# Two cross-attentions, fourth quarter of a context: another order of the projection units of the next context, and two of its loads and splits at other places

## The chip, the cores and the metric

The kernel runs on one core of one Trainium2 chip. The core has five engines that each work through a queue of their own: TensorE (PE: matmuls, and PEld: their weight loads), VectorE (DVE), ScalarE (ACT), GpSimd (POOL), and SyncE (SP), whose queue issues nearly all DMA transfers. They meet only through semaphores. An engine's queue is strictly in order, so an instruction that waits holds up all that stands behind it. The metric is the device time of one execution in microseconds (us); the median of three runs before is 2287.61 us (2285.31 to 2291.52).

## The reference

Two transformer layers over 8 inputs of 224 rows x 512, with one context of 750 x 512 per input. Each layer has a cross-attention and a feed-forward network, with gates:

```
x = x + tanh(g_xattn[0]) * attention0(layernorm(x), ctx)   # 16 heads of 32, no mask
x = x + tanh(g_ffn[0])   * bit_ffn(layernorm(x))           # ternary weights, depthwise convolution
x = x + tanh(g_xattn[1]) * attention1(layernorm(x), ctx, mask)   # 8 heads of 64, mask
x = x + tanh(g_ffn[1])   * fp4_ffn(layernorm(x))           # weights and activations rounded to FP4

# attention: q = x Wq, k = ctx Wk, v = ctx Wv
# out = softmax(q k^T * d^-0.5 [masked]) v Wo
```

All is float32 in the reference. The kernel keeps that precision with bf16 matmuls: each operand is the sum of a bf16 value (its high part) and a bf16 remainder (its low part), and a product takes three matmuls.

## The kernel before

The four stages run one after the other: attention 0 (to about 750 us), its feed-forward, attention 1 (from about 1130 to 1870 us), its feed-forward. One function, `cross_attention`, writes both attentions; `stacked` is true for attention 0 and false for attention 1. Here b is the number of an input with its context, and both have eight.

**Quarters and slots.** The work on b is cut into four quarters q = 0 to 3, with HC heads each (4 in attention 0, 2 in attention 1). Per head TensorE computes the transposed scores (`scores_t`, L1189) whose exponential feeds the values, the scores of the same head of the next input (`scores`, L1209, in two halves) of which VectorE takes the row maxima (L977, L972), and the values of the head two back (`values`, L1227). Between these stand the *units* that prepare later inputs, four slots per head: slot 0 ahead of `scores_t`, slot 1 behind it, slot 2 behind the values, slot 3 behind the second half of the scores. `quarter_units` lists the units of a quarter and `slots_of` gives each its slot; every engine's code calls both, so that all have the same order.

**Units.** ("X", s, b) transposes half s of the normalised input (L1161). ("K", (c, kh), b), ("Q", c, b) and ("V", j, b) project a chunk of the keys (for half kh of the context), of the queries, and a piece of the values (L1117). "M" transposes maxima, "OT" and "OP" are the output projection. Each unit passes three engines: TensorE computes it in one of two PSUM banks, ScalarE copies out the high part (`unit_hi_part`, L772 to L790), VectorE the low part (`unit_lo_part`), and only then does TensorE reuse the bank. In the fourth quarter of b the units are X, K and Q of b + 2: X(0), X(1), chunk 0 of the keys and of the queries. They are needed at the start of the next quarter, where head 0 of b + 2 gets its first scores.

**Keys and queries take a detour.** A head's rows must lie at other partitions than where the projection leaves them. When K(c, 1) or Q(c) is done, SP writes the chunk to DRAM (L466), waits until it has landed, and reads it back into the stack in three transfers (L476, `regroup`). SP does this unit by unit, in the order of the units. `scores` waits, at the first head of a quarter, for all six reads of its chunk (`st_in`).

**The context.** In attention 0 a context comes in two halves of 375 columns through one float32 buffer (L416, 750 KB). ScalarE rounds a half to bf16 (`split_ctx`, L737, waits for the load) and VectorE computes the remainders chunk by chunk (`split_chunk`, L918, at the places in CHUNKS). SP loads the second half behind the queries' regrouping in quarter 2. In attention 1 the halves come ready from DRAM (`load_parts`, L403, 750 KB each).

**ScalarE's other work.** For each head `exponentials` (L801) reads the banks of `scores_t`, and `exponentials_hi` (L811) rounds the result. TensorE may write the next head's transposed scores only when the exponential of the head before has read them (`exp_done`).

**Weight pieces.** Attention 1 also rounds the last stage's weights to FP4, one piece per quarter: SP stores the finished piece (L511) behind K(c, 1) and loads one (L503) behind Q(c).

Of the kernel before, what the change touches and what calls it, by code (L numbers as in the profile page):

```python
# [25 lines left out]
NJ = 6  # L26
# [68 lines left out]
def cross_attention(nc, tag, x_in, x_out, ctx_t, ctx_parts, weights, gate, masks, H, fp4_weights=None, kept=None):  # L95
# [16 lines left out]
    def quarter_units(q, b):  # L112
        kq = b + 1 if q < 3 else b + 2
        cc = (q + 1) % KC
        units = []
        if q == 3 and (b + 2).exists():
            units += [("X", 0, b + 2), ("X", 1, b + 2)]

        maxima = []
        if q == 2 and (b + 1).exists():  # L120
            maxima = [("M", 0, b + 1)]
        if q == 0 and b.exists() and b.number != 0:
            maxima = [("M", 1, b)]
        chunk = [("K", (cc, 0), kq), ("K", (cc, 1), kq), ("Q", cc, kq)] if kq.exists() else []
        if q == 1 and (b + -1).exists():

            units += [("OT", 0, b + -1), ("OT", 1, b + -1)] + chunk + [("OP", 0, b + -1), ("OP", 1, b + -1)]
        else:
            if stacked and q == 3 and chunk:
                units = chunk[:1] + units + [chunk[2], chunk[1]]  # L130
            else:
                units += chunk[:1] + maxima + chunk[1:] if stacked or q == 0 else maxima + chunk
        if (b + 1).exists():
            turn = ((0, 1, 2), (3,), (4, 5), ()) if stacked else ((0, 1), (2,), (3, 4, 5), ())
            units += [("V", j, b + 1) for j in turn[q]]
        return units

    def slots_of(q, b):

        units = quarter_units(q, b)  # L140
        use = (2, 0) if len(units) <= 2 * HC else (2, 0, 1, 3)
        open_slots = sorted(4 * j + k for j in range(HC) for k in use)
        slots = [[] for _ in range(4 * HC)]
        at = [open_slots[i * len(open_slots) // len(units)] for i in range(len(units))]
        if q == 0 and not stacked and units and units[-1][0] == "V":

            at = [0, 1, 2, 3, 6, 7] if len(units) == 6 else [0, 1, 3, 6, 7][5 - len(units):]
        if units and units[0][0] == "OT" and not stacked:
            at[:2] = [0, 1]
        if stacked and q == 3 and units:  # L150

            at = [1, 2, 4, 6, 9]
        for slot, u in zip(at, units):
            slots[slot].append(u)
        return slots
# [19 lines left out]
    with ExitStack() as ctx:  # L175
# [201 lines left out]
        def _(sp):  # L377
# [127 lines left out]
            def weight_pieces(q, b, unit):  # L505

                m = 4 * b.number + q - 2
                if unit[0] == "K" and unit[1][1] == 1 and 1 <= m <= FP4_PIECES:

                    sp.wait_ge(f_rounded, m + 1)  # L510
                    sp.dma_start(fp4_weights[m - 1][1], fw[:, (m - 1) % 2, :]).then_inc(fw_sent, 16)  # L511
                if unit[0] == "Q" and 1 <= m < FP4_PIECES - 1:

                    sp.wait_ge(fw_sent, m * 16)
                    load_weight_piece(m + 1)
# [29 lines left out]
            def quarter(q, b):  # L545
# [24 lines left out]
                for unit in quarter_units(q, b):  # L570
# [4 lines left out]
                        load_ctx(b + 2, 1)  # L575
                    if not stacked and q == 2 and (b + 2).exists():

                        if unit[:2] == ("K", (KC - 1, 1)):
                            load_ctx(b + 2, 0)
                        if unit[:2] == ("V", NJ - 1):  # L580
                            sp.wait_ge(unit_done, value(n))
# [135 lines left out]
        def _(act):  # L717
# [109 lines left out]
            def quarter(q, b):  # L827
# [6 lines left out]
                def unit_step(unit):  # L834
                    unit_hi_part(unit)
                    if stacked and unit[:2] == ("K", (KC - 1, 1)) and (b + 2).exists():
                        split_ctx(b + 2, 0, None)
                    if stacked and unit[:2] == ("K", (0, 0)) and (b + 2).exists():
                        split_ctx(b + 2, 1, None)

                for j in range(HC):
# [17 lines left out]
        def _(dve):  # L859
# [176 lines left out]
            def quarter(q, b):  # L1036
# [16 lines left out]
                for j in range(HC):  # L1053
# [24 lines left out]
                    for unit in slots[4 * j + 3]:  # L1078
                        unit_step(unit)

            CHUNKS = {(2, 3): [(0, 0), (0, 1)], (2, 4): [(0, 2), (0, 3)],
                      (3, 1): [(1, 0), (1, 1)], (3, 2): [(1, 2), (1, 3)]}
            MOMENTS = {(2, 0): 0, (2, 1): 1} if stacked else {(2, 0): 0}
            NORMALISED = {(2, 5): [0], (2, 7): [1]} if stacked else {(2, 2): [0], (2, 3): [1]}

# [16 lines left out]
        def _(pe):  # L1102
# [18 lines left out]
            def unit_products(unit):  # L1121
# [14 lines left out]
                if kind == "M":  # L1136

                    pe.wait_ge(sm_done, (b.index * H + (k + 1) * H2) * 2)
                if kind == "OP" and k == 0 or unit[:2] == ("Q", 0) and stacked and (b.number is None or b.number >= 2):

                    pe.wait_ge(unit_done, n - 1)
                elif not (isinstance(n, int) and n <= 2):
# [1383 lines left out]
```

## Time and profile before

| | |
|---|---|
| median of 3 runs | 2287.61 us (2285.31 to 2291.52) |
| profiled execution, device time | 2280.43 us |
| its span in the trace | 2278.6 us |
| TensorE matmuls / weight loads busy | 1975.2 us (87%) / 1385.9 us (61%) |
| VectorE, GpSimd, ScalarE busy | 1477.8, 1214.7, 949.6 us |
| TensorE granted clock, mean | 0.937 of full speed |

A row of a timeline gives the start in us from the span's start, how long the row lasts, the engine, the line, the operation with its output and inputs, how many instructions are merged in it, and in brackets how long the engine stood idle before it and what released it. Both attentions share names (`a_...`); the weights and keys of attention 1 are called `kept_w` and `kept_k`. A row of the waits gives who waited for whom, the total in us, how often, and the longest. A row of stretches gives each engine's busy time within a stretch, then the granted clock of TensorE, the busy share of the DMA engines, and their GB/s.

### The profile page before, as it was taken

The page shows a single profiled execution, that of the slowest core. Times are in us where ns is not written, and L with a number is a line of the kernel's source. Part 1 is how long each engine was busy: PE and PEld are TensorE (multiplying, and loading weights), DVE is VectorE, ACT ScalarE, POOL GpSimd, SP SyncE. Part 2 cuts the span into 40 slices and gives each one's busy share as a digit, 9 for nine tenths or more (in the row PEclk, how much of TensorE's full clock was granted, in tenths as well). Part 3 has the DMA queues.
Part 4 walks back from the last instruction along what each step waited for, and adds up shares of the span by engine and source line. Part 5 has one row for each costly group of instructions (what it writes and reads, how often), then busy time and mean ns, then how long its engine had stood idle before and what let it go on. Part 6 is the DMA issues. An engine that isn't in the chain of part 4 may idle for free. (4 is left out here: it accounts for less than half of the span.)

```text
span 2278.6 us, 42253 instructions
## 1 busy us (share of the span) xinstructions
PE 1975.2 (87%) x15208; PEld 1385.9 (61%) x15208; DVE 1477.8 (65%) x2752; ACT 949.6 (42%) x1289; POOL 1214.7 (53%) x1470
## 2 busy tenths in 40 slices
PE   5798898898897478989588898998999977899997
PEld 3466666666666367778355676666666664455553
DVE  4766666666656479897454556655656546898973
ACT  3266666666657573333133334334333443111111
POOL 4166666657756453333221556566666422777763
PEclk9899999999999589999788999999999988899998
DMA  7354344344331231111253443434444422011100
GB/s 208 94 123 107 92 108 118 94 112 119 96 92 41 99 97 33 40 32 33 86 162 93 114 124 116 135 118 136 123 127 132 127 83 65 28 33 33 36 23 28
DMA packets 184011, 208.67 MB, mean 92 GB/s; under 512 B 61480, under 2 KB 145704, under 8 KB 183336
## 3 DMA queue, kind: packets, MB, share of 16 engines
q1 hardware_dynamic: 183848, 206.46, 32.0%
q8 instruction: 107, 1.75, 0.3%
q14 instruction: 56, 0.46, 0.1%
HBM read 138.61 MB, written 67.53 MB: 90 GB/s over the span
## 5 line engine op out<-in xcount | busy, mean ns | idle before, releaser
L678 POOL TENSOR_TENSOR a_p_hl<-a_p,a_p_hl 125x448 bf16<-125x448 f32 x540 | 578.7, 1073 | 533.8 <-ACT a_p_hl L811 505.3
L811 ACT ACTIVATE a_p_hl<-a_p 125x1344 bf16<-125x1344 f32 x192 | 254.0, 1323 | 140.4 <-PE a_psum L1227 137.4
L801 ACT ACTIVATE a_p<-a_psum 125x1344 f32<-125x1344 f32 x192 | 247.7, 1290 | 130.5 <-PE a_psum L1189 123.0
L977 DVE TENSOR_REDUCE a_nm<-a_psum 112x1 f32<-112x750 f32 x256 | 236.4, 930 | 24.9 <-PE a_psum L1209 23.0
L1227 PEld LDWEIGHTS a_psum<-a_v_st,a_p_hl 125*128 125x128 bf16 x4608 | 185.4, 100 | 39.7 <-issue 19.7
L1227 PE MATMUL a_psum<-a_v_st,a_p_hl 125*128 125x65 bf16 (+2 forms) x4608 | 196.7, 198 | 9.5 <-ACT a_p_hl L811 3.1
L1209 PE MATMUL a_psum<-a_k_st,a_q_st 96*112 96x375 bf16 x512 | 134.0, 348 | 77.5 <-DVE a_nm L977 72.4
L1856 PE MATMUL f_conv<-f_u,f_taps 128*128 128x224 f32 x768 | 161.6, 360 | 22.2 <-DVE f_u L1708 21.3
L942 DVE TENSOR_TENSOR a_v_st<-a_psum,a_v_st 125x512 bf16<-125x512 f32 x96 | 66.4, 691 | 171.9 <-ACT a_v_st L779 171.9
L1117 PE MATMUL a_psum<-a_chl,kept_w 128*128 128x375 bf16 x768 | 141.9, 339 | 24.4 <-DVE kept_w L868 18.3
L1856 PEld LDWEIGHTS f_conv<-f_u,f_taps 128*128 128x128 f32 x768 | 141.9, 192 | 31.7 <-DVE f_u L1708 27.0
L1209 PE MATMUL a_psum<-kept_k,a_q_st 128*112 128x375 bf16 (+1 forms) x512 | 127.7, 350 | 38.4 <-DMA a_q_st<-a_q 35.6
L1117 PE MATMUL a_psum<-a_chl,a_w 128*128 128x375 bf16 x768 | 140.5, 335 | 18.9 <-DVE a_w L868 14.9
L972 DVE CUSTOM_DVE_ANT_0 a_psum<-a_psum,a_mask_b 112x750 f32<-112x750 f32 x128 | 120.0, 942 | 50.3 <-PE a_psum L1209 48.8
L936 DVE TENSOR_TENSOR a_k_tmp<-a_psum,a_k_tmp 128x375 bf16<-128x375 f32 x128 | 69.8, 545 | 125.5 <-ACT a_k_tmp L772 125.4
L779 ACT ACTIVATE a_v_st<-a_psum 125x512 bf16<-125x512 f32 x96 | 58.4, 608 | 208.7 <-PE a_psum L1117 208.7
L1117 PE MATMUL a_psum<-a_w,a_chl 128*125 128x512 bf16 x576 | 135.7, 386 | 3.2 <-DVE a_q_tmp L939 3.1
L1117 PE MATMUL a_psum<-kept_w,a_chl 128*125 128x512 bf16 x576 | 134.6, 384 | 3.5 <-DVE a_q_tmp L939 3.4
L772 ACT ACTIVATE a_k_tmp<-a_psum 128x375 bf16<-128x375 f32 x128 | 61.9, 484 | 170.8 <-PE a_psum L1117 168.3
L2181 POOL TENSOR_TENSOR f_ht<-f_ht,f_hp 128x512 f32<-128x512 f32 (+1 forms) x84 | 99.1, 1208 | 60.9 <-DVE f_hp L1934 59.8
L1587 ACT ACTIVATE f_t<-f_conv,f_cb 128x224 f32<-128x224 f32 x128 | 57.5, 449 | 167.0 <-PE f_conv L1856 167.0
L1117 PEld LDWEIGHTS a_psum<-a_chl,kept_w 128*128 128x128 bf16 x768 | 74.7, 102 | 79.4 <-issue 38.8
(251 smaller groups left out, 4045.5 us busy)
## 6 DMA issues: line engine op xcount, KB each, us to landing
a_k<-a_k_tmp SPq DMA_DIRECT2D x64, 375.0 KB, 2.9
a_k_st<-a_k SPq DMA_DIRECT2D x96, 187.5 KB, 3.4
kept_k<-a_k SPq DMA_DIRECT2D x96, 187.5 KB, 3.4
a_c<-in_ctx_t SPq DMA_DIRECT2D x16, 750.0 KB, 5.8
ctx_parts<-a_chl SPq DMA_DIRECT2D x16, 750.0 KB, 9.2
a_chl<-ctx_parts SPq DMA_DIRECT2D x16, 750.0 KB, 6.7
a_q_st<-a_q SPq DMA_DIRECT2D x192, 56.0 KB, 2.2
rounded<-a_fw SPq DMA_DIRECT2D x24, 352.0 KB, 3.7
```

The costliest lines, as they stand in the source:

```text
L678: ins = nc.gpsimd.tensor_tensor(p_hl[0:MC, h % 2, 1, cols], p32[0:MC, h % 2, cols], p_hl[0:MC, h % 2, 0, cols], ALU.subtract)
L801: nc.scalar.activation(p32[0:MC, par, :].rearrange("p (b n) -> p b n", b=3), st[0:MC, :, 0:2 * S], ACT.Exp, scale=scale).then_inc(exp_done, 1)
L811: nc.scalar.activation(p_hl[0:MC, par, 0, :], p32[0:MC, par, :], ACT.Copy).then_inc(phi_done, 1)
L936: ins = nc.vector.tensor_tensor(k_tmp[:, cc % 2, 1, cols], bank[:, 0:MK], k_tmp[:, cc % 2, 0, cols], ALU.subtract)
L942: ins = nc.vector.tensor_tensor(v_st[0:MC, b.parity, k, :, DK + 1:VW], bank[0:MC, :].rearrange("p (h d) -> p h d", h=H), v_st[0:MC, b.pari ...
L972: ins = nc.vector.tensor_tensor_reduce(out=sm_[0:HALF, 0:2, 0:MK], in0=sm_[0:HALF, 0:2, 0:MK], in1=mask_b[:, b.parity, s, :].rearrange("p ...
L977: ins = nc.vector.tensor_reduce(out, sm_[0:HALF, 0:2, 0:MK], AX.XY, ALU.max, negate=True)
L1117: ins = nc.tensor.matmul(out, lhs, rhs, start=(c == 0 and n == 0), stop=(c == KC - 1 and n == 2))
L1209: ins = nc.tensor.matmul(sm_[0:HALF, kh, 0:MK], q_stack(b.parity, at(h), rows)[:, s * HALF:(s + 1) * HALF], k_stack(b.parity, at(h), rows) ...
L1227: ins = nc.tensor.matmul(ob[:, c0:c0 + width], p_hl[0:MC, h % 2, part, j * S + Q0[s]:j * S + Q0[s] + P], v_st[0:MC, b.parity, j, h, 0:widt ...
L1856: ins = nc.tensor.matmul(conv[:, g % 2, c * S:(c + 1) * S], taps[:, g * GC + c, k, :], u[:, g % 2, c, k:k + S], start=(k == 0), stop=(k == 2))
L2181: ins = nc.gpsimd.tensor_tensor(ht[:, cols], ht[:, cols], hp[:, cols], op)
```

## The change

Four things move; no computation is added or removed.

- Attention 0, fourth quarter: the units were K(0,0), X(0), X(1), Q(0), K(0,1) and are K(0,0), X(0), K(0,1), X(1), Q(0), at the same slots 1, 2, 4, 6, 9.
- Attention 0: ScalarE's rounding of the second half of the context (L737) stands behind the last V unit of the third quarter, and VectorE's remainders of it one place earlier (behind the first and second maximum of head 12).
- Attention 1, fourth quarter: the units were X(0), X(1), K(0,0), K(0,1), Q(0) at slots 0, 1, 3, 4, 6 and are X(0), X(1), Q(0), K(0,0), K(0,1) at 0, 0, 2, 3, 4. Q(0) then waits until X(1) is wholly out of its bank, as in attention 0.
- Attention 1: SP loads the first half of the next context behind the queries of the third quarter, not behind its keys, and the weight piece that the fourth quarter loaded is loaded in the first quarter of the next, behind its unit K(1,0).

```diff
             if stacked and q == 3 and chunk:
-                units = chunk[:1] + units + [chunk[2], chunk[1]]
+                units = [chunk[0], units[0], chunk[1], units[1], chunk[2]]
+            elif q == 3:
+                units += chunk[2:] + chunk[:2]
             else:
                 units += chunk[:1] + maxima + chunk[1:] if stacked or q == 0 else maxima + chunk
...
+        if not stacked and q == 3 and units:
+
+            at = [0, 0, 2, 3, 4]
...
-                if unit[0] == "Q" and 1 <= m < FP4_PIECES - 1:
+                if q == 0:
+                    if unit == ("K", (1, 0), b + 1) and 2 <= m < FP4_PIECES:
+
+                        sp.wait_ge(fw_sent, (m - 1) * 16)
+                        load_weight_piece(m)
+                if unit[0] == "Q" and q != 3 and 1 <= m < FP4_PIECES - 1:
...
-                        if unit[:2] == ("K", (KC - 1, 1)):
+                        if unit[:2] == ("Q", KC - 1):
                             load_ctx(b + 2, 0)
...
-                    if stacked and unit[:2] == ("K", (0, 0)) and (b + 2).exists():
+                    if stacked and q == 2 and unit[:2] == ("V", NJ - 1) and (b + 2).exists():
                         split_ctx(b + 2, 1, None)
...
-                      (3, 1): [(1, 0), (1, 1)], (3, 2): [(1, 2), (1, 3)]}
+                      (3, 0): [(1, 0), (1, 1)], (3, 1): [(1, 2), (1, 3)]}
...
-                if kind == "OP" and k == 0 or unit[:2] == ("Q", 0) and stacked and (b.number is None or b.number >= 2):
+                if kind == "OP" and k == 0 or unit[:2] == ("Q", 0) and (b.number is None or b.number >= 2):
```

ScalarE in attention 0, from the last V unit of the third quarter (a_v_st) on. Before, the exponential (a_p) and rounding (a_p_hl) of head 11, the exponential of head 12 and K(0,0) (a_k_tmp) come ahead of the rounding of the context (a_chl):

```order
L779 ACTIVATE a_v_st<-a_psum 125x16x32
L796 REGISTER_ALU
L801 ACTIVATE a_p<-a_psum 125x1344
L807 REGISTER_ALU
L811 ACTIVATE a_p_hl<-a_p 125x1344
L796 REGISTER_ALU
L801 ACTIVATE a_p<-a_psum 125x1344
L765 REGISTER_ALU
L772 ACTIVATE a_k_tmp<-a_psum 128x375
L733 ISA
L737 ACTIVATE a_chl<-a_c 128x4x375
```

Now, from the same V unit on:

```order
L789 ACTIVATE a_v_st<-a_psum 125x16x32
L743 ISA
L747 ACTIVATE a_chl<-a_c 128x4x375
L806 REGISTER_ALU
L811 ACTIVATE a_p<-a_psum 125x1344
L817 REGISTER_ALU
L821 ACTIVATE a_p_hl<-a_p 125x1344
L806 REGISTER_ALU
L811 ACTIVATE a_p<-a_psum 125x1344
L775 REGISTER_ALU
L782 ACTIVATE a_k_tmp<-a_psum 128x375
```

The rounding of the context moved ahead of two exponentials, one rounding and one K unit.

TensorE in attention 0, from the unit X(0) on, before. `a_ident,a_xn` is X(0), then X(1), a_k_st,a_q_st are halves of the scores of heads 12 and 13, and `125x224 x6` are the transposed scores of head 13:

```order
L1161 MATMUL a_psum<-a_ident,a_xn 128x112 x4
L1209 MATMUL a_psum<-a_k_st,a_q_st 112x375 x2
L1161 MATMUL a_psum<-a_ident,a_xn 128x112 x4
L1189 MATMUL a_psum<-a_q_st,a_k_st 125x224 x6
L1209 MATMUL a_psum<-a_k_st,a_q_st 112x375 x2
```

and now, with K(0,1) (a_chl,a_w) there:

```order
L1171 MATMUL a_psum<-a_ident,a_xn 128x112 x4
L1219 MATMUL a_psum<-a_k_st,a_q_st 112x375 x2
L1127 MATMUL a_psum<-a_chl,a_w 128x375 x12
L1199 MATMUL a_psum<-a_q_st,a_k_st 125x224 x6
L1219 MATMUL a_psum<-a_k_st,a_q_st 112x375 x2
```

K(0,1) took the place of X(1), ahead of head 13; X(1) stands behind that head's values and Q(0), last, where K(0,1) was.

SP in attention 1, before, from the keys' reads of the third quarter (kept_k) to those of the fourth. `a_chl<-ctx_parts` is a load of half a context, `a_q<-a_q_tmp` and `a_q_st<-a_q` are the queries' write and reads:

```order
L476 DMA kept_k<-a_k 64x2x750 x3
L511 DMA rounded<-a_fw 128x704
L403 DMA a_chl<-ctx_parts 128x8x375
L466 DMA a_q<-a_q_tmp 128x2x224
L476 DMA a_q_st<-a_q 64x2x224 x3
L503 DMA a_fw<-in_w_up 128x704
L403 DMA a_chl<-ctx_parts 128x8x375
L466 DMA a_k<-a_k_tmp 128x2x750
L476 DMA kept_k<-a_k 64x2x750 x3
L511 DMA rounded<-a_fw 128x704
L466 DMA a_q<-a_q_tmp 128x2x224
L476 DMA a_q_st<-a_q 64x2x224 x3
```

and now:

```order
L481 DMA kept_k<-a_k 64x2x750 x3
L516 DMA rounded<-a_fw 128x704
L471 DMA a_q<-a_q_tmp 128x2x224
L481 DMA a_q_st<-a_q 64x2x224 x3
L508 DMA a_fw<-in_w_up 128x704
L408 DMA a_chl<-ctx_parts 128x8x375 x2
L471 DMA a_q<-a_q_tmp 128x2x224
L481 DMA a_q_st<-a_q 64x2x224 x3
L471 DMA a_k<-a_k_tmp 128x2x750
L481 DMA kept_k<-a_k 64x2x750 x3
L516 DMA rounded<-a_fw 128x704
```

The first context load moved behind the queries' reads and a weight piece, next to the second; the queries of chunk 0 moved ahead of its keys.

## Rows read from the trace of the kernel before

**Rows 1.** The page's first part: busy time, share of the span, instructions

```profile
PE 1975.2 (87%) x15208; PEld 1385.9 (61%) x15208; DVE 1477.8 (65%) x2752; ACT 949.6 (42%) x1289; POOL 1214.7 (53%) x1470
```

**Rows 2.** Waits of TensorE, 1300 to 1820 us (loop of attention 1)

```profile
PE a_psum L1209 <- DMA a_q_st<-a_q: 32.3, 13, 4.8
```

**Rows 3.** Waits of TensorE, 100 to 750 us (attention 0)

```profile
PE a_psum L1209 <- DVE a_nm L977: 60.6, 91, 2.2
...
PE a_psum L1209 <- DMA a_k_st<-a_k: 3.8, 3, 1.7
```

**Rows 4.** Timeline of TensorE, attention 1, two contexts

```profile
1310.40 2.71 PE L1117 MATMUL a_psum<-a_chl,kept_w 128*128 128x375 bf16 x12
...
1458.68 0.60 PE L1161 MATMUL a_psum<-a_ident,a_xn 112*128 112x112 f32 x4
...
1463.61 0.98 PE L1209 MATMUL a_psum<-kept_k,a_q_st 128*112 128x375 bf16 x4 [2.16 <-DMA a_q_st<-a_q]
...
1485.81 1.68 PE L1209 MATMUL a_psum<-kept_k,a_q_st 128*112 128x375 bf16 x4 [4.16 <-DMA a_q_st<-a_q]
```

**Rows 5.** Timeline of SP's DMA queue, the same context

```profile
1452.44 0.58 SPq L403 DMA_DIRECT2D a_chl<-ctx_parts  x1
1453.07 0.73 SPq L466 DMA_DIRECT2D a_q<-a_q_tmp  x1
1459.95 1.88 SPq L476 DMA_DIRECT2D a_q_st<-a_q  x3
...
1476.13 1.88 SPq L476 DMA_DIRECT2D kept_k<-a_k  x3
...
1478.69 0.43 SPq L466 DMA_DIRECT2D a_q<-a_q_tmp  x1
1482.19 1.88 SPq L476 DMA_DIRECT2D a_q_st<-a_q  x3
```

**Rows 6.** Timeline of VectorE, the same context, second half normalised

```profile
1460.11 0.54 DVE L893 TENSOR_SCALAR a_xn<-a_xin,a_mv,a_root 112x512 f32<-112x512 f32 x1
```

**Rows 7.** The keys' stack, 1300 to 1800 us: its 66 reads

```profile
DMA to landing us min/median/max: 3.0/3.4/3.9
```

**Rows 8.** Stretches, with PE, PEld, DVE, ACT, POOL, PEclk, DMA share, GB/s

```profile
353.24:361.05 7.81, 7.81 (x58) 6.09 (x59) 5.36 (x12) 3.02 (x4) 7.02 (x5) 0.61 0.07 17
1485.81:1489.29 3.48, 3.48 (x29) 2.39 (x30) 1.01 (x2) 0.00 (x0) 0.90 (x2) 0.52 0.66 220
```

**Rows 9.** Timeline of ScalarE and SP, attention 0, first, third and last context

```profile
162.45 0.66 SPq L416 DMA_DIRECT2D a_c<-in_ctx_t  x1
...
165.03 1.29 ACT L801 ACTIVATE a_p<-a_psum 125x1344 f32<-125x1344 f32 x1
...
343.05 1.29 ACT L801 ACTIVATE a_p<-a_psum 125x1344 f32<-125x1344 f32 x1
...
343.14 0.66 SPq L416 DMA_DIRECT2D a_c<-in_ctx_t  x1
...
348.58 1.45 ACT L737 ACTIVATE a_chl<-a_c 128x1500 bf16<-128x1500 f32 x1 [0.33 <-DMA a_c<-in_ctx_t]
...
607.81 0.63 SPq L416 DMA_DIRECT2D a_c<-in_ctx_t  x1
607.92 1.29 ACT L801 ACTIVATE a_p<-a_psum 125x1344 f32<-125x1344 f32 x1
```

**Rows 10.** The context's buffer, 100 to 650 us: its 12 loads

```profile
DMA to landing us min/median/max: 5.3/5.7/6.6
```

**Rows 11.** Timeline of TensorE, attention 0, third and fifth context

```profile
345.08 0.74 PE L1189 MATMUL a_psum<-a_q_st,a_k_st 99*125 99x224 bf16 x6
...
353.24 0.87 PE L1209 MATMUL a_psum<-a_k_st,a_q_st 96*112 96x375 bf16 x2 [2.01 <-DVE a_nm L977]
...
523.11 0.74 PE L1189 MATMUL a_psum<-a_q_st,a_k_st 99*125 99x224 bf16 x6
...
536.26 0.52 PE L1209 MATMUL a_psum<-a_k_st,a_q_st 96*112 96x375 bf16 x2
```

## The prediction

> **What bounds the kernel now.** I read the busy times first. TensorE's matmuls are busy for 87% of the span, the next engine, VectorE, for 65% [rows 1], and the share is higher still within the two attentions, whose loops run to about 750 us and from about 1200 to 1820 us. So TensorE's queue sets the pace there, and what counts is each gap in it and each spell at the lower clock.
>
> The list of waits then says whose gaps they are. In the loop of attention 1 TensorE waits 32.3 us, 13 times, for the copy that brings the queries into their stack, and for nearly nothing else [rows 2]. In attention 0 it waits 60.6 us for VectorE's row maxima in 91 short pieces, and only 3.8 us for the keys' copies [rows 3]. So attention 1 has something that a new order can win back, and attention 0 has little.
>
> The timeline of one context of attention 1 shows the two places [rows 4]. The scores of head 6 stand 2.16 us (place A) and those of the next context's head 0 stand 4.16 us (place B). The DMA queue explains both [rows 5]. At A the query write of chunk 3, issued at 1453.07 behind a 750 KB context load (1452.44), lands only at 1459.95, 6.9 us later, while the same write takes 3.5 us from 1478.69. At B the queries of chunk 0 are computed last: SP finishes the keys, then writes the queries at 1478.69, reads them back at 1482.19, and TensorE goes on at 1485.81.
>
> **The change in attention 1.** Six contexts of each attention have a fourth quarter with such units.
> - Place A. The query write now goes ahead of the load, at 1452.4. With the 3.5 us of the other write and the 3.6 us from the read's issue to TensorE's start (1482.19 to 1485.81), the queries are there at 1459.6, or at 1461 if the write shares the engines with the keys' copies; TensorE asks at 1463. The wait goes (2.16 us here, 5.9 us over six contexts).
> - The second transpose X1 moves ahead of head 6's transposed scores. X0 starts at 1458.68 and takes 0.5 us, but X1's input, VectorE's normalised half, is ready only at 1460.65 [rows 4, 6]. That is a new wait of 1.45 us, six times: +9 us. Behind it in TensorE's queue stand the scores for the exponential of head 6, and everything after.
> - Place B. The queries now come 9 us earlier, before both key units. The keys of chunk 0 are then last. To see when, I walked TensorE's queue with the durations of the trace at full clock: X1 ends at 1461.2, head 6's transposed scores take 1.8 us, its other scores twice 0.9, values 1.1, Q(0) 1.15 and each key unit 1.95, which puts the end of K(0,1) at 1470.75, some 1.2 us earlier than now. SP's three reads of the keys, issued at 1476.13 now, then start at 1474.9 and the last lands 4.7 us after that (1.3 us of issue and 3.4 us to landing [rows 7]), at 1479.6. TensorE, which has Q(0) no longer between, gets there at about 1479.2. The wait of 4.16 us becomes 0.3 to 1 us. I take 0.5, six times: +3 us against the 25.6 us removed (six waits of 3.8 to 4.8).
> - The clock. After place B TensorE runs 3.5 us at a granted 0.52 [rows 8], the lower level of 1.2 GHz, and part of the next key unit too: 2.71 us from 1310.40 where 2.08 is usual [rows 4]. That is 1.75 us and some 0.45 us, six times: -13 us if the wait is gone. At place A I leave the clock as it is, since the gap before X1 stands there instead.
> - The two context loads now follow each other at about 1459.0 and 1459.6 instead of 1452.4 and 1462.6, with a weight piece ahead. Together that is 1.85 MB; at the 220 GB/s of a stretch with copies [rows 8] it lasts 8.4 us, and by the walk K(0,0) needs the first half at 1466.9. I take +2 us in all (0 to +8). The next weight piece is loaded a quarter later in SP's order, behind the piece stored in this one; by the walk it lands about 1 us before VectorE asks, so it costs nothing, but its cover is thin.
>
> Sum: -31.5 (all thirteen waits but two small ones) - 13 + 9 + 3 + 2 = about -30 us, with -15 and -38 as ends.
>
> **The change in attention 0.** Here ScalarE's rounding of the second context half (one 1.45 us instruction, waiting for its load) moves from behind the K(0,0) unit of quarter 4 to behind the last V unit of quarter 3, ahead of head 11's exponential. SP's load isn't moved. It is issued at 343.14 [rows 9], while ScalarE ends that V unit just before its next instruction at 343.05, and a landing takes 5.3/5.7/6.6 us [rows 10]. Even at its old place ScalarE waited for it twice (0.33 us at 348.58). So ScalarE will stand idle 5.7 us, round for 1.4 us, and start head 11's exponential at 350.2 instead of 343.05. Behind it in ScalarE's queue are that head's rounding, head 12's exponential and the evictions of K(0,0) and X0. TensorE can't start head 12's transposed scores before that exponential has read the banks; it starts them at 345.08, 0.74 us after the exponential's end [rows 11]. The new wait is 343.14 + 5.7 + 1.4 - 343.05 - 0.74 = 6.4 us. The load's issue less the exponential's start is -2.58 us in the first context and -0.11 in the last [rows 9], and -5.2 us over six, so the sum is 6 x 6.36 - 5.2 = 33 us. With landings of 5.3 and 6.6 it is 31 and 38.
>
> Nothing of this comes back later. VectorE's maxima each wait for scores just made, so idle time before them stores nothing.
>
> Second, K(0,1) now stands at head 13's start and needs the rounded remainders of that half. VectorE makes them in four instructions of 0.5 us, two behind each maximum of head 12. From the start of head 12's transposed scores I walked the queue with the durations of the trace at full clock. K(0,0) ends at 2.5, head 12's second scores at 5.0, but VectorE, whose X0 part waits for ScalarE, ends the second maximum at 7.1 and the remainders at 8.1. K(0,1) thus waits 3 us; then comes X1 behind head 13's rounding, and Q(0) waits 1.5 us for it. Head 14's first scores start at 15.8 us. Before, this stretch takes 13.15 us at full clock (523.11 to 536.26) and 15.97 us with the lower clock (345.08 to 361.05) [rows 8, 11]. So +2.7 x 6 = 16 us at like clock; against the stretches as they are, some of them already slow, +7 if the clock then holds. I take +13. The queries' copy that now comes last is shorter than the keys', so the 3.8 us for a_k_st go.
>
> Sum: +33 + 13 - 4 = +42 us, with +32 and +55 as ends.
>
> **Total.** +42 - 30 = +12 us. The profiled execution took 2280.43 us (span 2278.6), 7 us under the median of 2287.61; on that median the forecast is 2300 us.
>
> **Two rules.** TensorE's clock after a gap: at 353.24, after 2.01 us without work, the trace shows 7.8 us at a granted 0.61 [rows 8]. The Trainium skill, "TensorE: Matmul & The Clock Gate", section "What's actually happening", says that the throttled clock is the default and activity releases it. By that rule a gap three times as long is followed by a slow stretch each time, which is the first rival below. Transfers: the query write behind the context load took 6.9 us, without it 3.5 [rows 5]. "DMA: Bandwidth & Descriptors", section "Issuing engines are not separate DMA queues", in the Trainium skill says that all DMAs run on the same 16 engines and interleave. By that rule the two halves of the context, now issued together, slow each other, which speaks against this edit and for the third rival.
>
> **The rivals.**
> - Lower clock after the new gap in attention 0. It adds the 3 us that the spell at 353.24 lost (7.8 us at 0.61), six times, to the forecast: +30, 2318 us. For it stands that spell [rows 8]. Against: much of that spell would lie beside the waits for VectorE. Chance 0.17.
> - Attention 0 costs only the new wait. The wait before K(0,1) merely replaces the one of 2.01 us that scores of head 13 have now [rows 11], and the landing is at its 5.3 us: 31 - 4 = +27, total -3, 2285 us. Chance 0.18.
> - Attention 1 gives half: keys' copies and context loads get in each other's way, so B keeps 2 us and K(0,0) waits 1 us; -15 instead of -30, 2315 us. Chance 0.15.
> - Faster: attention 0 absorbs the gap. VectorE, the engine waited for in 60.6 us, catches up while TensorE stands, and the next quarter's waits of 0.3 to 1.0 us go. This decides if they fall by over two thirds: a0 about +10, total -20, 2268 us. Against: those waits follow fresh scores. Chance 0.10.
> - That the queries' copy isn't what TensorE waits for can't be: all thirteen waits name it.
> - The forecast: 0.40, with 2293 to 2307 as its own range.
>
> A difference under 0.3% (6.9 us) can't be told from none. Slower by more: 0.33 of the forecast's 0.40, 0.17 and 0.15, so 0.65. Same: the forecast's other 0.07 and 0.15 of the second rival, so 0.22. Faster: 0.10 and that rival's last 0.03, so 0.13. The range of 2282 to 2320 leaves out the faster rival and the top of the first.
>
> **What would show it.** In attention 0 ScalarE's L747 (now L737) must show 5 us of idle time before it, released by the context load, and TensorE's transposed scores must wait about 6 us six times for ScalarE. K(0,1) must wait for VectorE's remainders. In attention 1 the 32.3 us for the query copies must nearly go, X1 must wait 1.4 us for the normalised half, and the waits at place B must name the keys' stack and stay under 1 us. Wrong it is if ScalarE's new wait stays under 3 us, or if TensorE's waits for VectorE in attention 0 fall by tens of us.

## The result: 2303 us, slower by 0.8%

| | before | changed |
|---|---|---|
| median, measured side by side (7 runs each) | 2285.31 us (2279.32 to 2291.52) | 2303.17 us (2300.41 to 2306.05) |
| ratio | | 1.0082, 95% interval 1.0065 to 1.0100 |
| profiled execution, its span | 2280.43, 2278.6 us | 2302.16, 2300.4 us |
| TensorE granted clock, mean | 0.937 | 0.932 |

The forecast was +12 us, 2300 us, with a chance of 0.65 for slower. The ratio makes it +18.8 us (+15 to +23). The difference of the two medians is 17.9 us, and the two profiled spans differ by 21.8 us; sums of waits from the traces are to be held against this last number.

Line numbers of the changed kernel are 10 higher than before from L737 on, those of SP's transfers 5 higher: the context rounding is L747, the exponential L811, the scores L1219, the transposed scores L1199, the projections L1127, the transposes of X L1171.

**Attention 0.** The waits of TensorE in its loop, 100 to 770 us; those of before are in [rows 3]:

```profile
PE a_psum L1219 <- DVE a_nm L987: 50.2, 87, 1.5
PE a_psum L1199 <- ACT a_p L811: 31.0, 6, 6.0
PE a_psum L1127 <- DVE a_chl L928: 18.6, 6, 3.3
PE a_psum L1127 <- DVE a_xnT L957: 7.2, 6, 1.4
```

Three waits are new, each six times: transposed scores for head 11's exponential, K(0,1) for VectorE's remainders, Q(0) for X1's. The wait for the keys' copies (a_k_st) is gone. The waits for maxima (a_nm) fell by some 10 us, because the new waits stand in place of some of them, such as the 2.01 us at head 13 [rows 11]. ScalarE's list and timeline show where the first comes from:

```profile
L747 ACT ACTIVATE a_chl<-a_c x12: 1452/1452/1456, 153.1 to 662.0; 128x1500 bf16<-128x1500 f32 x12
its engine sat idle before it (us, times) until:
  DMA a_c<-in_ctx_t: 27.3, 6
...
458.45 0.61 ACT L789 ACTIVATE a_v_st<-a_psum 125x512 bf16<-125x512 f32 x1 [2.30 <-PE a_psum L1127]
464.46 1.45 ACT L747 ACTIVATE a_chl<-a_c 128x1500 bf16<-128x1500 f32 x1 [5.39 <-DMA a_c<-in_ctx_t]
465.82 1.27 ACT L811 ACTIVATE a_p<-a_psum 125x1344 f32<-125x1344 f32 x1
```

ScalarE is done with the V unit at 459.07 and stands until the context half has landed; SP's queue issued that load only at 459.10:

```profile
459.10 0.64 SPq L421 DMA_DIRECT2D a_c<-in_ctx_t  x1
```

TensorE in the same context (the fourth of six), from head 12's transposed scores to head 14's first scores:

```profile
467.24 1.35 PE L1199 MATMUL a_psum<-a_q_st,a_k_st 99*125 99x224 bf16 x6 [6.02 <-ACT a_p L811]
468.38 3.97 PE L1127 MATMUL a_psum<-a_chl,a_w 128*128 128x375 bf16 x12
...
478.11 3.94 PE L1127 MATMUL a_psum<-a_chl,a_w 128*128 128x375 bf16 x12 [3.23 <-DVE a_chl L928]
481.85 1.33 PE L1199 MATMUL a_psum<-a_q_st,a_k_st 99*125 99x224 bf16 x6
...
487.00 1.32 PE L1127 MATMUL a_psum<-a_xnT,a_w 128*128 128x224 bf16 x12 [1.13 <-DVE a_xnT L957]
488.16 0.49 PE L1219 MATMUL a_psum<-a_k_st,a_q_st 96*112 96x375 bf16 x2
```

Both key units take 3.9 us where 2.08 is usual. Cut into four parts, this piece shows that the clock was low twice, once behind each gap. The granted clock is the third number from the end of a row:

```profile
467.24:473.00 5.76, 5.76 (x25) 3.60 (x26) 0.10 (x1) 2.98 (x3) 3.10 (x3) 0.50 0.02 4
473.50:476.50 3.00, 1.24 (x17) 0.68 (x13) 2.54 (x5) 1.75 (x2) 1.14 (x2) 1.00 0.00 0
477.00:483.50 6.50, 5.39 (x20) 3.37 (x21) 1.60 (x4) 0.77 (x2) 2.98 (x2) 0.50 0.00 0
484.00:488.16 4.16, 3.03 (x39) 2.60 (x36) 3.15 (x7) 3.44 (x4) 2.07 (x3) 1.00 0.48 154
```

While TensorE worked behind the first gap the clock came back to full, and while TensorE then stood for K(0,1) it fell again. All six contexts show these two slow spells.

I call the time from head 12's transposed scores to head 14's first scores *the stretch*. Read for all six contexts, it adds up to 88.4 us before (13.15 in the one context where the clock held) and 121.4 us now (18.8 to 21.0 each). The first and the last of the six starts, before and now:

```profile
167.06 0.74 PE L1189 MATMUL a_psum<-a_q_st,a_k_st 99*125 99x224 bf16 x6
...
609.95 0.74 PE L1189 MATMUL a_psum<-a_q_st,a_k_st 99*125 99x224 bf16 x6
```

```profile
173.52 1.35 PE L1199 MATMUL a_psum<-a_q_st,a_k_st 99*125 99x224 bf16 x6 [5.88 <-ACT a_p L811]
...
664.82 1.35 PE L1199 MATMUL a_psum<-a_q_st,a_k_st 99*125 99x224 bf16 x6 [4.22 <-ACT a_p L811]
```

Five periods took 442.9 us and take 491.3 us, so a context costs 9.7 us more. TensorE's first transpose of the feed-forward behind attention 0 moved from 795.86 to 853.19, before and now:

```profile
795.86 0.91 PE L1809 MATMUL f_xT_ps<-f_ident_b,f_xq 112*128 112x112 bf16 x8 [17.58 <-DVE f_xq L1657]
```

```profile
853.19 0.91 PE L1819 MATMUL f_xT_ps<-f_ident_b,f_xq 112*128 112x112 bf16 x8 [17.66 <-DVE f_xq L1667]
```

So attention 0 lost 57.3 us, and what follows it won 57.3 - 21.8 = 35.5 us.

**Attention 1.** The waits of TensorE in its loop, 1330 to 1840 us, which is all of the list; before, 32.3 us for the query copies stood there [rows 2]:

```profile
PE a_psum L1171 <- DVE a_xn L903: 8.5, 6, 1.4
PE a_psum L1219 <- DMA kept_k<-a_k: 4.3, 6, 1.6
```

Place B of one context, and a stretch of 100 us (busy time of PE, PEld, DVE, ACT, POOL, then the granted clock): the wait of 4.16 us [rows 4] is 0.63, and the clock is at 1.00.

```profile
1443.01 0.98 PE L1219 MATMUL a_psum<-kept_k,a_q_st 128*112 128x375 bf16 x4 [0.63 <-DMA kept_k<-a_k]
```

```profile
1450.00:1550.00 100.00, 97.81 (x804) 69.02 (x803) 65.23 (x153) 43.53 (x52) 68.57 (x83) 1.00 0.46 133
```

### The profile page after: what moved, and what is told of

Read it like the earlier page. It is cut to its first block and busy times, and to the rows that moved or that the text cites. A ratio compares the mean times of both kernels' runs of the same rounds, so it can differ in the third digit from the quotient of the medians.

```text
span 2300.4 us, 42253 instructions
## 1 busy us (share of the span) xinstructions
PE 1979.1 (86%) x15208; PEld 1386.0 (60%) x15208; DVE 1479.5 (64%) x2752; ACT 951.1 (41%) x1289; POOL 1208.3 (53%) x1470
## 5 line engine op out<-in xcount | busy, mean ns | idle before, releaser
L688 POOL TENSOR_TENSOR a_p_hl<-a_p,a_p_hl 125x448 bf16<-125x448 f32 x540 | 572.5, 1061 | 572.0 <-ACT a_p_hl L821 543.7
L811 ACT ACTIVATE a_p<-a_psum 125x1344 f32<-125x1344 f32 x192 | 247.5, 1289 | 127.4 <-PE a_psum L1199 121.2
L1237 PEld LDWEIGHTS a_psum<-a_v_st,a_p_hl 125*128 125x128 bf16 x4608 | 179.4, 99 | 38.3 <-issue 18.8
L1237 PE MATMUL a_psum<-a_v_st,a_p_hl 125*128 125x65 bf16 (+2 forms) x4608 | 189.9, 195 | 8.8 <-issue 2.9
L1127 PE MATMUL a_psum<-a_chl,a_w 128*128 128x375 bf16 x768 | 159.3, 366 | 36.9 <-DVE a_chl L928 18.6
L1219 PE MATMUL a_psum<-a_k_st,a_q_st 96*112 96x375 bf16 x512 | 133.9, 349 | 60.4 <-DVE a_nm L987 60.1
L1127 PE MATMUL a_psum<-a_chl,kept_w 128*128 128x375 bf16 x768 | 136.7, 331 | 22.8 <-DVE kept_w L878 18.0
L1127 PEld LDWEIGHTS a_psum<-a_chl,a_w 128*128 128x128 bf16 x768 | 82.3, 109 | 98.6 <-issue 42.5
L1199 PE MATMUL a_psum<-a_q_st,a_k_st 99*125 99x224 bf16 x768 | 109.3, 285 | 36.1 <-ACT a_p L811 36.0
L1127 PE MATMUL a_psum<-kept_w,a_chl 128*125 128x512 bf16 x576 | 136.3, 387 | 3.5 <-DVE a_q_tmp L949 3.4
L1127 PE MATMUL a_psum<-a_w,a_chl 128*125 128x512 bf16 x576 | 133.9, 383 | 2.8 <-DVE a_q_tmp L949 2.7
L1219 PE MATMUL a_psum<-kept_k,a_q_st 128*112 128x375 bf16 (+1 forms) x512 | 123.3, 341 | 8.5 <-DMA kept_k<-a_k 4.3
```

The lines of the kernel that those rows point to most:

```text
L688: ins = nc.gpsimd.tensor_tensor(p_hl[0:MC, h % 2, 1, cols], p32[0:MC, h % 2, cols], p_hl[0:MC, h % 2, 0, cols], ALU.subtract)
L811: nc.scalar.activation(p32[0:MC, par, :].rearrange("p (b n) -> p b n", b=3), st[0:MC, :, 0:2 * S], ACT.Exp, scale=scale).then_inc(exp_done, 1)
L1127: ins = nc.tensor.matmul(out, lhs, rhs, start=(c == 0 and n == 0), stop=(c == KC - 1 and n == 2))
L1199: ins = nc.tensor.matmul(out, k_stack(b.parity, at(h), rows)[:, j * MC:(j + 1) * MC], q_stack(b.parity, at(h), rows), start=(t == 0 and no ...
L1219: ins = nc.tensor.matmul(sm_[0:HALF, kh, 0:MK], q_stack(b.parity, at(h), rows)[:, s * HALF:(s + 1) * HALF], k_stack(b.parity, at(h), rows) ...
L1237: ins = nc.tensor.matmul(ob[:, c0:c0 + width], p_hl[0:MC, h % 2, part, j * S + Q0[s]:j * S + Q0[s] + P], v_st[0:MC, b.parity, j, h, 0:widt ...
```

## The experiments

Times are medians; the ratio to the kernel before, measured beside it, stands with its 95% interval. The kernel before had 2287.72, 2287.92 and 2281.14 us in the three groups of runs.

### Each attention alone

Edit `e_a1`: attention 1's edits only. The three places of attention 0 are put back:

```diff
-                units = [chunk[0], units[0], chunk[1], units[1], chunk[2]]
+                units = chunk[:1] + units + [chunk[2], chunk[1]]
...
-                    if stacked and q == 2 and unit[:2] == ("V", NJ - 1) and (b + 2).exists():
+                    if stacked and unit[:2] == ("K", (0, 0)) and (b + 2).exists():
...
-                      (3, 0): [(1, 0), (1, 1)], (3, 1): [(1, 2), (1, 3)]}
+                      (3, 1): [(1, 0), (1, 1)], (3, 2): [(1, 2), (1, 3)]}
```

> Only the four edits of attention 1 on the kernel before; attention 0 as it was. Theory A (read from the two traces: attention 1's loop is 34 us shorter after the change, attention 0 and what lies around it 56 us longer): 2285 - 34 = 2251 us. Theory B (the sizes forecast, -30 for attention 1 and +42 for attention 0, and the other 10 us of the result from somewhere else): 2255 us. If attention 1 gained only half: 2270 us.

Edit `e_a0`: those three places as in the changed kernel, attention 1 as before.

> Only the edits of attention 0 (unit order, ScalarE's rounding of the second context half early, remainders one place earlier); attention 1 as before. Theory A: 2285 + 56 = 2341 us. Theory B: 2285 + 42 = 2327 us. With this and the kernel that has only attention 1's edits, the two differences should add up to the +18 to +22 us of both together; if they don't, the parts touch each other.

| | median | ratio | difference |
|---|---|---|---|
| e_a1 | 2246.29 us | 0.9830 (0.9810 to 0.9849) | -39 us (-43 to -35) |
| e_a0 | 2341.63 us | 1.0244 (1.0222 to 1.0263) | +56 us (+51 to +60) |

The sum, +17, fits the +18.8 of both together: within some 5 us, the width of these intervals, the parts don't touch each other. A later repeat of `e_a1` gave 0.9853 (0.9833 to 0.9873), -34 us. Attention 0 is past the end of my range for it (+32 to +55), attention 1 at the end of its own (-15 to -38).

### Attention 0: which of its edits costs what

Edit `e_split`: the kernel before, and only ScalarE's rounding early.

```diff
-                    if stacked and unit[:2] == ("K", (0, 0)) and (b + 2).exists():
+                    if stacked and q == 2 and unit[:2] == ("V", NJ - 1) and (b + 2).exists():
                         split_ctx(b + 2, 1, None)
```

> On the kernel before, only ScalarE's rounding of the second context half is moved to behind the last V unit of the third quarter; attention 0's unit order and VectorE's places as before, attention 1 as before. The new wait is there (about 31 us over six contexts), no unit waits for the remainders. Theory of the wait alone: +31 - 4 to +31, so 2312 to 2316 us, with the granted clock after the gap near 1. Theory of the clock: the gap is followed by some 10 us or more at 0.6 to 0.7 and costs 3 to 4 us more per context, so +50, 2335 us.

Measured: 2326.84 us, 1.0171 (1.0144 to 1.0198), +39 us. The waits in attention 0's loop:

```profile
PE a_psum L1209 <- DVE a_nm L977: 56.5, 95, 1.5
PE a_psum L1189 <- ACT a_p L801: 36.2, 9, 7.7
PE a_psum L1209 <- DMA a_k_st<-a_k: 11.0, 6, 3.0
```

The wait for the exponential is there: 35.0 us in the six contexts (the other 1.2 us stand at the end of attention 0, where the kernel before has such waits too). The wait for the keys' copies grew from 3.8 to 11.0. The time lies between my two theories. The stretch adds nothing, it takes 88.6 us in sum, as before: the 4.0 us more at the exponential and the 7.2 us more at the keys' copies are what stands against the part over 31 us. One context shows how the stretch stays as long. The clock is low behind the new wait and full again 5 us later, and the wait at head 13, which had a slow spell behind it before (2.01 us [rows 8, 11]), is now 0.89 us without one:

```profile
370.80:377.00 6.20, 6.17 (x48) 4.15 (x48) 0.73 (x2) 3.23 (x4) 3.10 (x3) 0.63 0.01 1
377.00:385.60 8.60, 6.84 (x73) 5.36 (x72) 7.46 (x15) 6.36 (x7) 7.17 (x5) 1.00 0.01 2
```

So one slow spell took the place of another, and this run doesn't tell what a slow spell costs; `e_fill` below does.

Edit `e_order`: the kernel before with attention 0's new unit order and VectorE's remainders one place earlier, ScalarE's rounding still behind K(0,0) (`e_a0` without the line of `e_split`).

> On the kernel before, attention 0 with the new unit order and VectorE's remainders one place earlier, but ScalarE's rounding of the second half stays behind K(0,0); attention 1 as before. Theory A (two separate causes): the 31 us wait of the transposed scores is gone, the wait of K(0,1) for the remainders (about 3 us, six times) and the low clock behind it stay, so the stretch from head 12's transposed scores to head 14's first scores is some 17 to 20 us instead of 14.7 on average: +15 to +30, less 4 for the keys' copies, 2299 to 2314 us. Theory B (the clock falls only because of the long wait ahead): the stretch is 15.7 us, +6 - 4, 2290 us.

Measured: 2300.10 us, 1.0064 (1.0043 to 1.0084), +15 us by the ratio and +12 by the medians. Theory A holds at its low end: the stretch adds up to 112.6 us (18.0 to 19.5 each) though no long wait stands ahead of it. K(0,1)'s wait (3.45 to 4.52 us) is enough to bring the low clock:

```profile
PE a_psum L1117 <- DVE a_chl L918: 22.6, 6, 4.5
PE a_psum L1117 <- DVE a_xnT L947: 7.3, 6, 1.3
...
363.78 3.44 PE L1117 MATMUL a_psum<-a_chl,a_w 128*128 128x375 bf16 x12 [4.52 <-DVE a_chl L918]
```

VectorE's timeline shows what K(0,1) waits for. Two remainder instructions stand behind each maximum, so chunks 2 and 3 come behind X0's low part and the second maximum, although ScalarE's rounding (L737) had ended 3 us before:

```profile
359.69 1.01 DVE L918 TENSOR_TENSOR a_chl<-a_c,a_chl 128x375 bf16<-128x375 f32 x2 [1.02 <-ACT a_chl L737]
361.33 0.62 DVE L947 TENSOR_TENSOR a_xnT<-a_psum,a_xnT 128x448 bf16<-128x448 f32 x1 [0.63 <-ACT a_xnT L782]
361.88 0.93 DVE L977 TENSOR_REDUCE a_nm<-a_psum 112x1 f32<-112x750 f32 x1
362.72 1.00 DVE L918 TENSOR_TENSOR a_chl<-a_c,a_chl 128x375 bf16<-128x375 f32 x2
```

Of the stretch's +24.2 us, 3.8 come back because the keys' copies are no longer last. By the medians and the ratio some 5 to 8 more are missing; by the trace only 2.3, since the feed-forward's first transpose starts 18.1 us later than before. That difference stays open. The early rounding and the new order together are 39 + 15 = 54, against 56 for `e_a0`: nearly additive, as two separate slow spells would be. The early rounding is the greater part.

### Attention 0: the wait or the clock

Edit `e_fill`: the changed kernel, TensorE kept at work in the two new gaps. The inputs stay as late as they are, and part of each gap holds matmuls whose result the next unit overwrites.

```diff
+            def filler(b, times):
+                n = units.base + units.k + 1
+                bank = banks[:, (units.start + units.k + 1) % 2, :]
+                pe.wait_ge(ctx_split, b.index * 2 + 1)
+                pe.wait_ge(unit_done, n - 2)
+                for _ in range(times):
+                    project(bank[:, 0:MK], 1, slice(0, P), chl, slice(0, MK))
...
                     h = q * HC + j
+                    if stacked and q == 3 and (b + 2).exists() and j < 2:
+                        filler(b + 2, 2 - j)
```

> The changed kernel, with TensorE kept at work in the two new waits of attention 0: it computes the product of the unit K(0,0) twice more ahead of head 12's transposed scores, and once more ahead of K(0,1), into the bank that the next unit overwrites (36 extra matmuls per context, nothing else changed). The waits for ScalarE and VectorE stay as late as they are. Theory that only the waiting costs: same time as the changed kernel, 2303 us, or a few us more. Theory that the low clock behind the gaps costs as much again: the stretch from head 12's transposed scores to head 14's first scores falls from 20.9 to about 16 us, up to -30 us, 2273 us; half of that is 2288.

Measured: 2285.59 us, 0.9995 (0.9982 to 1.0008), 18 us less than the changed kernel by the medians and 20 by the two ratios (they ran in different groups), with 216 more matmuls. TensorE in the context where the clock held throughout:

```profile
360.08 3.98 PE L1127 MATMUL a_psum<-a_chl,a_w 128*128 128x375 bf16 x24
365.79 0.76 PE L1208 MATMUL a_psum<-a_q_st,a_k_st 99*125 99x224 bf16 x6 [1.73 <-ACT a_p L811]
...
373.77 2.09 PE L1127 MATMUL a_psum<-a_chl,a_w 128*128 128x375 bf16 x12 [0.86 <-DVE a_chl L928]
...
380.27 1.32 PE L1127 MATMUL a_psum<-a_xnT,a_w 128*128 128x224 bf16 x12 [1.30 <-DVE a_xnT L957]
381.43 0.49 PE L1228 MATMUL a_psum<-a_k_st,a_q_st 96*112 96x375 bf16 x2
```

That stretch is 15.64 us, all at full clock; my walk had said 15.8. The six add up to 104.6 us instead of 121.4, so 16.8 us came back in the stretch, near the 18 to 20 of the time. (The trace, taken from the slowest of the twelve executions, shows attention 0 13.4 us shorter than in the changed kernel.) In the other five the filler left 2.4 to 3.4 us of the wait open, and the clock was still low for a while (17.3 to 18.6 us each). At 15.64 each it would be 93.8: by this the low clock costs the changed kernel 27.6 us in the stretch, where it cost the kernel before 9.5 (88.4 - 6 x 13.15).

### Attention 1: the clock, the loads and X1's wait

Edit `e_fill_b`: the kernel before, and in attention 1's first quarter two products of a key unit (24 matmuls) ahead of the scores of the next context's head 0, at place B (`filler` as above, without the wait for the context).

```diff
+                    if not stacked and q == 0 and j == 0 and b.number != 0 and (b + 1).exists():
+                        filler(b)
                     if (b + 1).exists():
                         scores(b + 1, h, 0)
```

> The kernel before, with TensorE kept at work while it waits for the query copies at place B of attention 1: two extra products of a key unit (24 matmuls, about 3.9 us at full clock) ahead of the scores of the next context's head 0, into the bank that the next unit overwrites. The copies come as late as before. It measures the clock term of attention 1 by itself. Theory of the forecast: -13 us (six times 2.2 us), 2275 us. Theory that attention 1's larger gain (-39 to -41 instead of -30) is clock: -20 us or more, 2267 us. If the clock costs nothing: 2288 us.

Measured: 2268.80 us, 0.9935 (0.9912 to 0.9958), -15 us (-20 to -10), though the copies come as late as ever. At place B:

```profile
1479.79 4.00 PE L1117 MATMUL a_psum<-a_chl,kept_w 128*128 128x375 bf16 x24
1484.02 0.98 PE L1217 MATMUL a_psum<-kept_k,a_q_st 128*112 128x375 bf16 x4 [0.23 <-DMA a_q_st<-a_q]
```

The scores take 0.98 us where they took 1.68 [rows 4]. So the clock term of attention 1 is about 15 us by the ratio, 12 by the medians, and 11 by the trace, where place B returns every 86.5 us instead of 88.4; I had 13.

Edits `e_a1_order` and `e_a1_load` part the unit order from the moved transfers. `e_a1_order` is `e_a1` with the first context half loaded behind the keys again; `e_a1_load` is the kernel before with only the two moved transfers.

```diff
-                        if unit[:2] == ("Q", KC - 1):
+                        if unit[:2] == ("K", (KC - 1, 1)):
                             load_ctx(b + 2, 0)
```

> Attention 1's edits alone, but the first half of the next context is again loaded behind the keys of the third quarter, ahead of the queries' write. Theory: place A's wait (2.16 us at one of the contexts, 5.9 us over six) stays, place B's is gone: 2246 + 6 = 2252 us, a few us more if the clock falls behind it. Rival: the load's place is worth nothing, since the late queries' copy is absorbed: 2246 us.

> On the kernel before, only the two moved transfers of attention 1 (the first half of the next context behind the queries of the third quarter, the fourth quarter's weight piece a quarter later); unit order as before. Theory: place A's wait goes (-6 us), place B's of 25.6 us stays with its low clock: 2282 us. Rival: the two context halves now follow each other and come late, or share the engines with the copies at place B: 2288 us or more.

Measured: `e_a1_order` 2251.40 us, 0.9844 (0.9817 to 0.9872); `e_a1_load` 2284.85 us, 0.9983 (0.9963 to 1.0004). The order is nearly all of the gain. The loads' place is worth 3 to 5 us by the medians of each pair, which neither interval can tell from nothing; against the repeat of `e_a1` (0.9853) it is nothing at all. The traces show a size of 4: waits for copies in attention 1 (1220 to 1830 us) are 7.9 us in `e_a1` and 11.8 us in `e_a1_order`:

```profile
PE a_psum L1219 <- DMA kept_k<-a_k: 4.3, 5, 1.6
PE a_psum L1219 <- DMA a_q_st<-a_q: 3.6, 2, 3.3
```

```profile
PE a_psum L1219 <- DMA kept_k<-a_k: 7.2, 6, 3.2
PE a_psum L1219 <- DMA a_q_st<-a_q: 4.6, 3, 3.1
```

The forecast of 5.9 us for this run was not met where it was expected: of the added 3.9 us only 1.0 stands at the query copies. At place A they are waited for once in the six contexts, 0.95 us, right behind X1's wait of 1.42 us, which may have covered the rest; no run tests this apart. The other 2.9 us stand at the keys' copies.

Edit `e_a1_norm`: `e_a1`, and VectorE normalises both halves of the next input in a row.

```diff
-            NORMALISED = {(2, 5): [0], (2, 7): [1]} if stacked else {(2, 2): [0], (2, 3): [1]}
+            NORMALISED = {(2, 5): [0], (2, 7): [1]} if stacked else {(2, 2): [0, 1]}
```

> Attention 1's edits alone, and VectorE normalises the second half of the next input right behind the first, behind head 5's first maximum, where it stood idle. If X1's wait of 1.4 us is a loss of its own, the six waits (8.5 us) go: 2246 - 8 = 2238 us. Rival: the wait only moves on, to Q(0), which needs X1 out of its bank, and nothing is won: 2246 us.

> The kernel with attention 1's edits and both halves normalised together, once more beside the others, for a direct comparison on one chip: 2238 us if X1's wait was a net loss of 8 us, 2243 to 2246 us if half or more of it is given back to the waits for the copies, which its first trace shows.

> The kernel with attention 1's edits alone, once more on the same chip as the other three: 2246 us. The difference to the one with both halves normalised together tells what X1's wait is worth.

| | first group | repeat |
|---|---|---|
| e_a1 | 2246.29 us, 0.9830 (0.9810 to 0.9849) | 2248.03 us, 0.9853 (0.9833 to 0.9873) |
| e_a1_norm | 2244.84 us, 0.9812 (0.9786 to 0.9838) | 2237.35 us, 0.9806 (0.9783 to 0.9829) |

The wait of X1 is gone from the list. The gain is 11 us in the repeat, where both ran on one chip and the intervals just part, and 4 us by the first ratios, where they overlap. X1's wait was a loss of its own; whether all of its 8.5 us comes back is not settled. This is the fastest kernel of the study, 44 us under the kernel before.

### Attention 0 of before: keeping its clock up

Edit `e_best_fill`: `e_a1_norm` with six extra matmuls (about 1 us) ahead of head 13's first scores in attention 0's fourth quarter, where TensorE waits for VectorE (`filler` with the first two of the four chunks of the product).

```diff
+                    if stacked and q == 3 and j == 1 and (b + 2).exists():
+                        filler(b + 2)
                     if (b + 1).exists():
                         scores(b + 1, h, 0)
```

> Attention 1's edits with both halves normalised together (2244.8 us), and in attention 0, old order, six extra matmuls (half a key product, about 1 us) ahead of the first scores of head 13 of the fourth quarter, where TensorE waits 1.6 to 2.2 us for VectorE and in four of six contexts then runs at the lower clock. If a gap shortened to under 1.2 us keeps the clock up, the six stretches fall from 88.4 us to about 79 us: 2244.8 - 9 = 2236 us. Rival: the extra work delays VectorE's next maxima or the clock falls all the same: 2245 us.

Measured: 2240.28 us, 0.9808 (0.9784 to 0.9832), no gain over the 2237.35 beside it. The clock did what was expected: the stretch is 13.14 to 13.16 us in all six contexts, 78.9 us in sum against 85.6. But five periods take 443.9 us, and 443.2 without the filler. The waits for the keys' copies tell where it went, first this kernel and then `e_a1`, whose attention 0 is that of before:

```profile
PE a_psum L1230 <- DMA a_k_st<-a_k: 8.4, 6, 1.9
```

```profile
PE a_psum L1219 <- DMA a_k_st<-a_k: 2.4, 2, 2.0
```

With K(0,1) last, as in the old order, its copy leaves and returns some time after the unit. What TensorE gains ahead (6.7 us in the stretch) shows up as a wait for that copy (6.0 us more). The same waits grew in `e_split` (11.0 us).

## Why the prediction was right, and where its sizes were off

The direction, the waits and their places were read rightly. That the total came so near is partly luck, as the third and fourth points below say.

| term | forecast | measured | from |
|---|---|---|---|
| attention 0: wait for the exponential | +33 | +31.0 | waits |
| attention 0: stretch, work at like clock | +16 (part of 13) | +14.9 | 6 x (15.64 - 13.15) |
| attention 0: stretch, clock | -3 (the rest of 13) | +18.2 | 33.1 - 14.9 (33.1 = 121.4 - 88.4) |
| attention 0: keys' copies | -4 | -3.8 | waits |
| attention 0, all | +42 | +57 (trace), +56 (alone) | |
| attention 1: waits | -31.5 + 9 + 3 = -19.5 | -32.3 + 8.5 + 4.3 = -19.5 | waits |
| attention 1: clock | -13 | -15 (-20 to -10) | e_fill_b |
| attention 1: context loads | +2 | none in the list of waits | |
| attention 1, all | -30 | -35.5 (trace), -39 and -34 (alone) | |
| together | +12 | +18.8 (spans 21.8) | |

- **The early rounding was read rightly.** A load issued at 459.10 behind ScalarE's V unit, a wait of 5.39 us for it, and 4.1 to 6.0 us of TensorE's time in each of six contexts: the step stood as written, 31.0 for 33. `e_split` shows it alone (35.0).
- **The remainders too.** K(0,1) waits 2.8 to 3.3 us (I had 3) and Q(0) 1.1 to 1.4 us (1.5). The stretch at full clock is 15.64 us for 15.8.
- **The term that was mis-sized is the one I took at 13.** I had +16 at like clock, and +7 if the clock then holds; what happened is the reverse. The clock was low twice within the stretch, and the term measured +33. The argument that failed stands in the first rival: "much of that spell would lie beside the waits for VectorE". In the context shown above TensorE has 11.5 us of matmuls at half speed, a loss of 5.75 us, and the stretch is 5.3 us longer than the 15.64 at full clock: the waits covered next to nothing. A likely reason, argued and not tested, is that each maximum waits for scores just made. The first rival's mechanism was therefore real, at a chance of 0.17. It had one slow spell per context and put the term at 13 + 18 = 31; there were two, and it measured 33. The rule of "What's actually happening" in "TensorE: Matmul & The Clock Gate" of the Trainium skill, by which activity releases the lower clock, agrees with this trace: the clock is back at full after 6 us of work behind the first gap, and again after 5.5 us of work behind the second.
- **The total came near 2300 and not the rival's 2318 by luck.** With the stretch at +33 and all else as forecast, the time would have been 2320 us, the end of the range. Attention 1 won 5 us more than forecast, the rounding's wait cost 2 less, and some 3 us of attention 0's terms (60 in sum, 57 in the trace) came back outside them. None of the three was foreseen as a counterweight. That gives the 21.8 us of the spans; the median is another 3 to 4 us lower.
- **Attention 1 went as forecast,** place by place: the thirteen waits gone, X1's 1.42 us, place B's down to 0.37 to 1.56 us (one of the six over the 1 us that I allowed) and named kept_k. The load that shares the engines with a query write cost less than the 5.9 us that I took from the trace of before: put back in `e_a1_order`, it raises the waits for copies by 3.9 us, and the time by no more than its noise. "Issuing engines are not separate DMA queues" in "DMA: Bandwidth & Descriptors" of the Trainium skill says that all transfers share the 16 engines. The trace of before agrees: a query write took 6.9 us behind the load and 3.5 us without it [rows 5]. But the rival that I hung on it (attention 1 gives half) fell, since no wait for the context halves is in the list.

## What to carry to other kernels

Before an instruction is moved ahead of others in an engine's queue, read when its input is issued and landed: an early place that waits for a transfer holds up everything behind it, here 31 us for a rounding of 1.45 us. Price a new gap on TensorE twice, as the wait and as the slow spell behind it, and do so for each gap by itself: here the second gap brought a slow spell of its own, after the clock had come back. And a gain ahead of a copy that takes its own time is no gain: look which transfer the next stage waits for before winning clock ahead of it.

## What the runs showed of the hardware

- Filling a gap with useless matmuls made the program faster by 15 us (`e_fill_b`, ratio) and 18 us (`e_fill`, medians), and by nothing where the next wait was a transfer (`e_best_fill`).
- The length of a gap alone doesn't tell whether the clock falls. Behind 2.01 us in the kernel before, 7.8 us ran at a mean of 0.61 [rows 8, 11]. Behind the six waits of 1.42 us at X1 in the changed kernel it fell once, 1.1 us after the work had resumed. Behind 3.06 us in one context of `e_fill` the clock was low from the first matmul on (transposed scores of 1.35 us); behind 3.07 us in another these still ran at full clock (0.76 us), and it fell 0.8 us after the work had resumed, so that the key unit took 3.75 us where 2.08 is usual:

```profile
460.24 1.35 PE L1208 MATMUL a_psum<-a_q_st,a_k_st 99*125 99x224 bf16 x6 [3.06 <-ACT a_p L811]
...
557.80 0.76 PE L1208 MATMUL a_psum<-a_q_st,a_k_st 99*125 99x224 bf16 x6 [3.07 <-ACT a_p L811]
558.40 3.75 PE L1127 MATMUL a_psum<-a_chl,a_w 128*128 128x375 bf16 x12
```
